# Two-layer graph network on one core: additions between the layers moved behind the next quotient, and two waits put inside GpSimd's groups of gathers

## The chip, the cores and the metric

The kernel runs on one core of one Trainium2 chip. A core has five engines that run their own instruction streams and meet only at semaphores: TensorE (PE), VectorE (DVE), ScalarE (ACT), GpSimd (POOL) and SyncE (SP), which here only issues DMAs. The metric is the device time of one execution in microseconds (us), lower is better.

## The reference

A graph has 6250 nodes with 128 features and 106250 edges sorted by their target node; every node has an edge to itself. Two layers run one after the other, each on the layer-normed and rectified nodes:

```
h = relu(layernorm(x))
# layer 0, per edge and feature
msg = h[src] + edge_attr
e = exp(beta*msg - segment_max(beta*msg, dst)[dst])
agg = segment_sum(msg * e / segment_sum(e, dst)[dst], dst)
x = x + (agg @ H + bias + h)            # H from phm_rule and W
# layer 1, four heads of 32 features
Wx = h @ W.T
logit = leaky_relu(Wx[src].a_left + Wx[dst].a_right, 0.2)
out = segment_sum(softmax_by_dst(logit) * Wx[src], dst)
x = x + elu(out)
```

## The kernel before, in words

The edges are cut into 208 groups of 512 (four blocks of 128 edges, one edge on each partition). Both layers are a software pipeline over the groups. Each engine runs the same list of stages, every stage with a fixed lag in groups; `sweep` (line 17) writes the first groups out, then a loop that is unrolled over 8 groups (`RING`), then the last ones. Nothing plans the order at run time: each engine does its instructions as written and waits at semaphores that count finished groups.

**Layer 0, group g.** GpSimd issues four indirect DMAs (`gather0`, line 655), which fetch the rows `h[src]` from DRAM into one of four buffers `ring_h` (`HRING` = 4). Before the first block it waits until ScalarE has lifted group g-4 out of that buffer (`lifted`). ScalarE copies the rows to PSUM (`lift0`, line 811), VectorE adds the edge features that SyncE has loaded (`add0`, line 1135), TensorE transposes the sum (`turn0`, line 1392), VectorE runs a scan forward and one backward for the maximum of each target node (`maxima0`, lines 1112 and 1117), and TensorE turns the maxima back and subtracts them in PSUM (`unturn0`, lines 1398 and 1402, two groups behind `turn0`). The end of `unturn0` increments `unturned`. ScalarE takes exponentials, VectorE the products, TensorE multiplies by one-hot matrices (line 1383) to sum over the target nodes, and ScalarE merges the sums into `acc`.

**Between the layers** the 6250 nodes are 13 batches of 512 (the last has 106). For batch b GpSimd makes a near quotient (`near0`), ScalarE copies it to PSUM (`lift_near0`, line 830), and VectorE finishes the division (`quotient0(b)`, line 1171, which increments `mid_agg`). TensorE multiplies by H (`layer_out(b)`, lines 1435 and 1440), one batch after the other into two PSUM places: it waits for `mid_agg` of its batch and for `self_res` of batch b-2. VectorE then adds the result to the nodes (`finish0(b)`, line 1177, which increments `self_res`) and takes the statistics for the next layernorm (four instructions of line 963). `lift_near0(b)` waits for the quotient of batch b-2, and GpSimd's `near0(b)` for the lift of batch b-4. Then VectorE makes the normed rows (`above1`), TensorE the products with W (`layer_in`, line 1462), and SyncE stores them to DRAM.

**Layer 1, group g.** GpSimd gathers from that table (`gather1`, line 683) into eight buffers; VectorE forms the logits when the four blocks have landed (`logits1`, line 1258); TensorE transposes them one group later (`turn1`, line 1492, which increments `msgT`); VectorE scans for the maxima; the rest is as before. VectorE also makes the one-hot matrices (`one_hot1`, line 1096).

In this text "block 2 of group g" is the third gather of a group, since blocks count from 0.

Of the kernel before, what the change touches and what calls it, by code (L numbers as in the profile page):

```python
# [44 lines left out]
def apart(eng):  # L45


    eng.nop(nofuse=True)


def later(item, n):

    return not isinstance(item, int) or item >= n


def gnn_kernel(nc, x_in, src_in, dst_in, ea_in, rule_in, w0_in, bias_in, beta_in, w1_in, a_in, out):
# [15 lines left out]
    NBAT = -(-NT // GB)  # L72
# [18 lines left out]
    with ctx:  # L91
# [225 lines left out]
        L0, L1 = layer_sems(0), layer_sems(1)  # L317
# [27 lines left out]
        def logs(b):  # L345
            if b < SPARE_LOGS:
                return (pos, elu_e, fin)[b // 2][:, b % 2, :]
            return onehot[:, b - SPARE_LOGS, :, :].rearrange("p b n -> p (b n)")
# [4 lines left out]
        def near_bank(b):  # L353
            return bank[b % 2]
# [21 lines left out]
        def real_rows(g, b):  # L376
            if isinstance(g, int) and g == NG - 1:
                return max(0, min(P, E - (g * GE + b * P)))
            return P
# [7 lines left out]
        def last(stage, back, **where):  # L387
            g = NG - 1 - back
            stage(g, g % RING, g // RING, **where)
# [197 lines left out]
        def _(pool):  # L587
# [52 lines left out]
            def gather0(g, s, use):  # L640
                if isinstance(g, int) and g < HALF:
                    pool.wait_ge(first_src, 16)
                    if g == 2:
                        pool.wait_ge(key_out, len(TABLE_BANKS))
                elif s < HALF:
                    pool.wait_ge(L0["listed"][0], 16 * use)
                else:
                    pool.wait_ge(L0["listed"][1], 16 * (use + 1))
                if later(g, HRING):
                    pool.wait_ge(L0["lifted"], g - (HRING - 1))  # L650
                apart(pool)
                for b in range(GB):
                    n = real_rows(g, b)
                    if n:
                        pool.indirect_dma_start(hg[0:n, s % HRING, b, :], None, h_dram,  # L655
                                                bass.IndirectOffsetOnAxis(ap=meta_g[0:n, s, b:b + 1], axis=0)
                                                ).then_inc(L0["gathered"][s % HRING], 16)

            sweep_edges(pool, [(0, gather0)])

            pool.wait_ge(pool_sum, len(POOL_SUMS))
# [13 lines left out]
            def gather1(g, s, use):  # L675
                pool.wait_ge(L1["listed"][s // HALF], 16 * (use + 1))
                if later(g, RING):
                    pool.wait_ge(L1["multiplied"], g - (RING - 1))
                apart(pool)
                for b in range(GB):  # L680
                    n = real_rows(g, b)
                    if n:
                        pool.indirect_dma_start(msg[0:n, s, b, :], None, wx_dram,  # L683
                                                bass.IndirectOffsetOnAxis(ap=meta_g[0:n, s, b:b + 1], axis=0)
                                                ).then_inc(L1["gathered"][s], 16)

            for u in range(WXB):
                pool.wait_ge(wx_stored[u], 16 * ((NBAT - 1 - u) // WXB + 1))
            sweep_edges(pool, [(0, gather1)])


# [255 lines left out]
        def _(dve):  # L947
# [218 lines left out]
            def quotient0(b):  # L1166
                w = LAST if b == NBAT - 1 else GE
                dve.wait_ge(mid_quot, b + 1)
                dve.wait_ge(mid_lifted, b + 1)
                rows = logs(b)[:, 0:w]  # L1170
                dve.scalar_tensor_tensor(rows, near_bank(b)[:, 0:w], 2.0, rows, ALU.subtract, ALU.mult).then_inc(mid_agg, 1)

            def finish0(b):
                t, rows = extent(b)
                dve.wait_ge(mid_out, b + 1)
                tiles = nodes[0:rows, b * GB:b * GB + t, :]
                dve.tensor_tensor(tiles, tiles, sums[0:rows, 1, b % 2, 0:t * D].rearrange("p (t d) -> p t d", d=D), ALU.add
                                  ).then_inc(self_res, 1)
                dve.wait_ge(self_res, b + 1)
                statistics(b)  # L1180
# [8 lines left out]
            last(products0, 1)  # L1189
            quotient0(0)  # L1190
            last(products0, 0)
            quotient0(1)
            dve.wait_ge(dve_sum, len(DVE_SUMS))
            dve.wait_ge(pool_sum, len(POOL_SUMS))
            quotient0(2)
            quotient0(3)
            for b in range(NBAT):
                if b + 4 < NBAT:
                    quotient0(b + 4)
                finish0(b)  # L1200
            dve.wait_ge(measured, 2 * NBAT)

# [355 lines left out]
```

## Time and profile before

| what | value |
|---|---|
| time, median of 3 runs | 2254.29 us (2253.85 to 2254.93) |
| the profiled execution's own time | 2258.94 us |
| its span, first to last instruction | 2257.2 us |
| layer 0, first to last gather's start | 36.97 to 1075.76 us |
| layer 1, first to last gather's start | 1165.09 to 2209.11 us |
| TensorE, VectorE, ScalarE, GpSimd busy | 86%, 88%, 63%, 73% |

The share of busy time is an average; which engine bounds a stage is read from who waits for whom in it. A row of the timeline gives the start in us from the span's start, the busy time in us, engine, line, operation, output and inputs, and in square brackets the idle time of that engine just before it and what ended it.

### The profile page before, as it was taken

How to read it: one execution, taken by the hardware profiler on the slowest of the kernel's cores; microseconds unless marked ns; L12 is line 12 of the kernel's file. 1: busy time of each engine (PE TensorE's matmuls, PEld its weight loads, DVE VectorE, ACT ScalarE, POOL GpSimd, SP SyncE). 2: the span in 40 equal slices, each digit the busy share in tenths (PEclk: the TensorE clock that was granted, in tenths of full speed). 3: DMA queues.
4: the chain of work that ended last, by engine and by line, in shares of the span. 5: the costliest groups of instructions: out<-in, count | busy, mean ns of one | idle time of the engine just before them, and what ended most of it. 6: DMA issues, size and time to landing. Idle time of an engine off the chain costs nothing.

```text
span 2257.2 us, 61657 instructions
## 1 busy us (share of the span) xinstructions
PE 1940.5 (86%) x14541; PEld 1712.6 (76%) x14542; DVE 1986.2 (88%) x3873; ACT 1419.4 (63%) x3494; POOL 1644.8 (73%) x1739
## 2 busy tenths in 40 slices
PE   2888888888888888888879999999999899899997
PEld 1777777777777767777768888888888888888886
DVE  7999999999999999999759889888888888888886
ACT  3677777776777677777635555555555555555556
POOL 5777777777777777777527777777777777777775
PEclk9999999999999999999768989999999999999998
DMA  6444444444444444443023333333333333333331
GB/s 214 128 126 137 132 132 136 123 132 132 137 132 132 128 133 132 133 136 112 6 81 61 60 59 59 59 58 59 59 59 58 58 59 59 59 59 59 58 59 68
DMA packets 318697, 213.52 MB, mean 95 GB/s; under 512 B 169938, under 2 KB 279074, under 8 KB 318642
## 3 DMA queue, kind: packets, MB, share of 16 engines
q0 software_dynamic: 53184, 112.31, 20.8%
q1 hardware_dynamic: 264608, 100.15, 17.1%
q8 instruction: 23, 0.38, 0.1%
q10 hardware_dynamic: 850, 0.43, 0.1%
q14 instruction: 32, 0.26, 0.0%
HBM read 200.69 MB, written 10.29 MB: 93 GB/s over the span
## 4 chain that ended last, share of the span: by engine, by line
POOL 45%; issue 21%; DMA 13%; DVE 9%; PE 5%; ACT 5%; SPq 1%; ACTq 1%; POOLq 1%; DVEq 0%
POOL msg L683 25%; POOL ring_h L655 19%; DMA ring_h<-h_dram,meta_g 10%; DMA msg<-wx_dram,meta_g 3%; DVE seg_max L1117 2%; DVE sums L1112 2%; ACT banks L811 2%; PE sums L1383 1%; DVE onehot L1096 1%; PE sums L1440 1%; DVE prod L1281 1%; ACT acc L777 1%; SPq L556 1%; POOL wgt L703 0%; ACT sums L797 0%
## 5 line engine op out<-in xcount | busy, mean ns | idle before, releaser
L683 POOL DMA_INDIRECT msg<-wx_dram,meta_g x831 | 791.8, 953 | 304.4 <-issue 246.1
L655 POOL DMA_INDIRECT ring_h<-h_dram,meta_g x831 | 786.6, 947 | 265.7 <-issue 244.8
L1383 PE MATMUL sums<-onehot,prod 128*128 128x128 f32 x3296 | 686.4, 292 | 17.7 <-issue 5.9
L1383 PE MATMUL sums<-onehot,wgt 128*128 128x128 f32 x3296 | 668.9, 286 | 0.0
L1383 PEld LDWEIGHTS sums<-onehot,prod 128*128 128x128 f32 x3296 | 531.1, 203 | 52.0 <-issue 51.2
L1383 PEld LDWEIGHTS sums<-onehot,wgt 128*128 128x128 f32 x3296 | 532.5, 203 | 0.0
L777 ACT ACTIVATE acc<-sums 128x1022 f32 x410 | 419.9, 1024 | 0.1
L811 ACT ACTIVATE banks<-ring_h,sign 128x512 f32<-128x512 f32 x208 | 143.9, 692 | 266.8 <-DMA ring_h<-h_dram,meta_g 259.2
L1402 PEld LDWEIGHTS sums<-neg_ident,seg_max 128*128 128x128 f32 x1664 | 220.1, 193 | 100.5 <-issue 100.0
L1392 PE MATMUL banks<-ident,msg 128*128 128x128 f32 x832 | 137.4, 288 | 160.0 <-DVE msg L1135 159.9
L1112 DVE TENSOR_TENSOR_SCAN sums<-flags,seg_max,banks 4x512 f32<-4x512 bf16 x207 | 264.1, 1276 | 5.8 <-PE banks L1492 4.0
L1112 DVE TENSOR_TENSOR_SCAN banks<-flags,seg_max,banks 128x512 f32<-128x512 bf16 x207 | 264.6, 1278 | 0.0
L1117 DVE TENSOR_TENSOR_SCAN seg_max<-flags,banks 128x512 f32<-128x512 bf16 x208 | 253.9, 1221 | 7.2
L1117 DVE TENSOR_TENSOR_SCAN seg_max<-flags,sums 4x512 f32<-4x512 bf16 x208 | 251.2, 1208 | 7.1
L1392 PEld LDWEIGHTS banks<-ident,msg 128*128 128x128 f32 x832 | 89.0, 142 | 198.1 <-issue 182.7
L769 ACT ACTIVATE carried<-acc,scale 128x2 f32 x414 | 121.3, 293 | 170.7 <-PE sums L1383 147.2
L1402 PE MATMUL sums<-neg_ident,seg_max 128*128 128x128 f32 x1664 | 220.7, 276 | 0.0
L1483 PEld LDWEIGHTS banks<-window,onehotT 128*128 128x128 f32 x1664 | 211.4, 199 | 9.3 <-issue 9.3
L1135 DVE SCALAR_TENSOR_TENSOR msg<-msg,sign,banks 128x512 f32<-128x512 f32 x208 | 155.3, 747 | 71.3 <-ACT banks L811 60.4
L1398 PE MATMUL sums<-msg,ident 128*128 128x512 f32 x416 | 215.1, 599 | 1.9 <-ACT sums L797 1.8
L1483 PE MATMUL banks<-window,onehotT 128*128 128x4 f32 x1664 | 205.6, 247 | 8.3 <-DMA window<-wx_dram 7.9
L902 ACT ACTIVATE sums<-logit_d 128x16 f32<-128x16 f32 x208 | 39.0, 188 | 260.4 <-DVE logit_d L1273 258.2
(215 smaller groups left out, 2887.4 us busy)
## 6 DMA issues: line engine op xcount, KB each, us to landing
msg<-in_edge_attr SPq DMA_DIRECT2D x207, 256.0 KB
flags<-flag_dram SPq DMA_DIRECT2D x52, 512.2 KB
window<-wx_dram SPq DMA_DIRECT2D x832, 2.0 KB
ring_h<-h_dram,meta_g POOLq DMA_INDIRECT x831
msg<-wx_dram,meta_g POOLq DMA_INDIRECT x831
wx_dram<-msg SPq DMA_DIRECT2D x13, 272.0 KB, 2.1
nodes<-in_x SPq DMA_DIRECT2D x6, 512.0 KB, 6.5
h_dram<-acc SPq DMA_DIRECT2D x12, 256.0 KB
```

Source lines behind the costliest of these rows:

```text
L655: pool.indirect_dma_start(hg[0:n, s % HRING, b, :], None, h_dram, bass.IndirectOffsetOnAxis(ap=meta_g[0:n, s, b:b + 1], axis=0)).then_inc( ...
L683: pool.indirect_dma_start(msg[0:n, s, b, :], None, wx_dram, bass.IndirectOffsetOnAxis(ap=meta_g[0:n, s, b:b + 1], axis=0)).then_inc(L1["ga ...
L777: act.activation(acc[:, :, bass.ds(node + 1, WIN - 1)], where[:, :, 1:WIN], ACT.Copy).then_inc(k["merged"], 1)
L811: act.activation(row_psum, ring_h[:, s % HRING, :], ACT.Copy, scale=sign[:, 0:1]).then_inc(L0["lifted"], 1)
L1112: dve.tensor_tensor_scan(run, flag[:, 0:GE], data, before, ALU.add, ALU.max).then_inc(k["scanned"], 1)
L1117: dve.tensor_tensor_scan(seg_max[0:n, par, ::-1], flag[:, GE:0:-1], run[:, ::-1], -BIG, ALU.add, ALU.max).then_inc(k["scanned"], 1)
L1135: dve.scalar_tensor_tensor(msg[:, s, :, 0:D], msg[:, s, :, 0:D], sign[:, 0:1], row_psum.rearrange("p (b d) -> p b d", b=GB), ALU.mult, ALU.add
L1383: ins = pe.matmul(where[:, j, bass.ds(off, P)], what[:, slot, b, :], onehot[:, s, b, :], start=(b == 0), stop=(b == GB - 1), skip_group_ch ...
L1392: ins = pe.transpose(bank[s % 2][:, b * P:(b + 1) * P], msg[:, s, b, 0:D], ident[:, :])
L1398: pe.matmul(shift_psum.rearrange("p (b d) -> p b d", b=GB), ident[:, :], msg[:, s, :, 0:D], start=True, stop=False, skip_group_check=True)
L1402: ins = pe.matmul(shift_psum[:, b * P:(b + 1) * P], seg_max[:, s % 2, b * P:(b + 1) * P], neg_ident[:, :], start=False, stop=(b == GB - 1) ...
L1483: ins = pe.matmul(bank[1][:, b * H:(b + 1) * H], onehotT[:, s % 2, b * P:(b + 1) * P], window[:, s, b, :], start=True, stop=True)
```

## The change

Three edits. In layer 0, from group 4 on, GpSimd waits before block 2 of group g until TensorE has finished `unturn0` of group g-4. In layer 1, from group 2 on, it waits before block 3 of group g until TensorE has finished `turn1` of group g-2. Each wait is followed by an empty instruction (`apart`), which keeps it from being joined to the DMA. Between the layers VectorE no longer makes four quotients ahead of the first `finish0`: it makes one, and then `quotient0(b + 1)` and `finish0(b)` in turn.

```diff
                 for b in range(GB):
+                    if b == 2 and later(g, 4):
+                        pool.wait_ge(L0["unturned"], g - 3)
+                        apart(pool)
                     n = real_rows(g, b)
...
                 for b in range(GB):
+                    if b == 3 and later(g, 2):
+                        pool.wait_ge(L1["msgT"], g - 1)
+                        apart(pool)
                     n = real_rows(g, b)
...
             last(products0, 0)
-            quotient0(1)
             dve.wait_ge(dve_sum, len(DVE_SUMS))
             dve.wait_ge(pool_sum, len(POOL_SUMS))
-            quotient0(2)
-            quotient0(3)
             for b in range(NBAT):
-                if b + 4 < NBAT:
-                    quotient0(b + 4)
+                if b + 1 < NBAT:
+                    quotient0(b + 1)
                 finish0(b)
```

GpSimd in the loop of layer 0, before: the end of one group of gathers and the next group. `lifted0` and `unturned0` are the semaphores of layer 0, `listed0_0` that of the index lists.

```order
L650 REGISTER_ALU [waits listed0_0]
L655 DMA ring_h<-h_dram,meta_g 128x128 [waits lifted0]
L655 DMA ring_h<-h_dram,meta_g 128x128 x3
L650 REGISTER_ALU [waits listed0_0]
L655 DMA ring_h<-h_dram,meta_g 128x128 [waits lifted0]
L655 DMA ring_h<-h_dram,meta_g 128x128 x3
```

The same place of the changed kernel (its lines are 3 to 6 further down):

```order
L650 REGISTER_ALU [waits listed0_0]
L658 DMA ring_h<-h_dram,meta_g 128x128 [waits lifted0]
L658 DMA ring_h<-h_dram,meta_g 128x128
L658 DMA ring_h<-h_dram,meta_g 128x128 [waits unturned0]
L658 DMA ring_h<-h_dram,meta_g 128x128
L650 REGISTER_ALU [waits listed0_0]
L658 DMA ring_h<-h_dram,meta_g 128x128 [waits lifted0]
L658 DMA ring_h<-h_dram,meta_g 128x128
```

The order of the gathers is the same; the third of each four has a wait of its own.

VectorE between the layers, before: the first two rows are `quotient0(0)` and the last product of layer 0, `pos`, `elu_e` and `fin` rows of line 1171 are the quotients of batches 1 to 4.

```order
L1171 SCALAR_TENSOR_TENSOR pos<-banks,pos 128x512 [waits mid_lifted,mid_quot]
L1147 TENSOR_TENSOR prod<-sums,msg 128x512 [waits weighed0,summed0]
L1171 SCALAR_TENSOR_TENSOR pos<-banks,pos 128x512 [waits mid_lifted,mid_quot]
L1171 SCALAR_TENSOR_TENSOR elu_e<-banks,elu_e 128x512 [waits mid_quot,mid_lifted,pool_sum,dve_sum]
L1171 SCALAR_TENSOR_TENSOR elu_e<-banks,elu_e 128x512 [waits mid_lifted,mid_quot]
L1171 SCALAR_TENSOR_TENSOR fin<-banks,fin 128x512 [waits mid_lifted,mid_quot]
L1177 TENSOR_TENSOR nodes<-nodes,sums 128x512 [waits mid_out]
L963 BN_STATS stats<-nodes 128x6 [waits self_res]
```

The same place of the changed kernel, where line 1177 is now the quotient and line 1183 the addition of `finish0`:

```order
L1177 SCALAR_TENSOR_TENSOR pos<-banks,pos 128x512 [waits mid_lifted,mid_quot]
L1153 TENSOR_TENSOR prod<-sums,msg 128x512 [waits weighed0,summed0]
L1177 SCALAR_TENSOR_TENSOR pos<-banks,pos 128x512 [waits mid_quot,mid_lifted,pool_sum,dve_sum]
L1183 TENSOR_TENSOR nodes<-nodes,sums 128x512 [waits mid_out]
L969 BN_STATS stats<-nodes 128x6 [waits self_res]
L969 BN_STATS stats<-nodes 128x6 x3
L1177 SCALAR_TENSOR_TENSOR elu_e<-banks,elu_e 128x512 [waits mid_lifted,mid_quot]
L1183 TENSOR_TENSOR nodes<-nodes,sums 128x512 [waits mid_out]
```

The first addition stands behind the quotient of batch 1 instead of that of batch 4, and from there on quotients and additions alternate, three batches closer together than before.

## Rows read from the trace of the kernel before

**Rows 1.** The page, busy us (share of the span) of each engine

```profile
PE 1940.5 (86%) x14541; PEld 1712.6 (76%) x14542; DVE 1986.2 (88%) x3873; ACT 1419.4 (63%) x3494; POOL 1644.8 (73%) x1739
```

**Rows 2.** Groups by line, GpSimd: busy us, mean ns, idle before and its enders

```profile
L655 POOL DMA_INDIRECT ring_h<-h_dram,meta_g x831 | 786.6, 947 | 265.7 <-issue 244.8 <-DMA h_dram<-acc 12.6 <-ACT banks L811 7.9
L683 POOL DMA_INDIRECT msg<-wx_dram,meta_g x831 | 791.8, 953 | 304.4 <-issue 246.1 <-DMA wx_dram<-msg 51.2 <-DVE prod L1281 7.0
```

**Rows 3.** The waits: us in total, times, longest us

```profile
ACT banks L811 <- DMA ring_h<-h_dram,meta_g: 259.2, 197, 3.5
...
POOL msg L683 <- issue: 246.1, 807, 0.3
POOL ring_h L655 <- issue: 244.8, 803, 0.3
```

**Rows 4.** Timeline of GpSimd, layer 0: block 2 of groups 4, 39, 200

```profile
60.15 0.94 POOL L655 DMA_INDIRECT ring_h<-h_dram,meta_g  x1 [0.30 <-issue]
...
235.24 0.95 POOL L655 DMA_INDIRECT ring_h<-h_dram,meta_g  x1 [0.30 <-ACT banks L811]
...
1040.74 0.95 POOL L655 DMA_INDIRECT ring_h<-h_dram,meta_g  x1 [0.31 <-issue]
```

**Rows 5.** Timeline of TensorE, layer 0: end of unturn0, groups 0, 35, 196

```profile
61.26 1.91 PE L1402 MATMUL sums<-neg_ident,seg_max 128*128 128x128 f32 x8
...
234.29 1.59 PE L1402 MATMUL sums<-neg_ident,seg_max 128*128 128x128 f32 x8
...
1038.87 1.05 PE L1402 MATMUL sums<-neg_ident,seg_max 128*128 128x128 f32 x8
```

**Rows 6.** Timeline of GpSimd, layer 1: block 3 of group 9

```profile
1214.10 0.94 POOL L683 DMA_INDIRECT msg<-wx_dram,meta_g  x1 [0.30 <-issue]
```

**Rows 7.** Timeline of TensorE, layer 1: turn1 of group 7

```profile
1212.63 0.60 PE L1492 MATMUL banks<-ident,logit 128*4 128x128 f32 x4
```

**Rows 8.** Timeline of TensorE between the layers: layer_out 0 to 3, 12, first turn_h

```profile
1098.01 0.38 PE L1435 MATMUL sums<-bias_rows,ones_rows 3*128 3x512 bf16 x1
...
1100.39 0.38 PE L1435 MATMUL sums<-bias_rows,ones_rows 3*128 3x512 bf16 x1
...
1104.68 0.38 PE L1435 MATMUL sums<-bias_rows,ones_rows 3*128 3x512 bf16 x1 [1.84 <-DVE nodes L1177]
...
1107.16 0.60 PE L1435 MATMUL sums<-bias_rows,ones_rows 3*128 3x512 bf16 x1
...
1131.46 0.34 PE L1435 MATMUL sums<-bias_rows,ones_rows 3*106 3x128 bf16 x1
...
1135.28 1.97 PE L1451 MATMUL banks<-ident,hn 128*128 128x128 f32 x8 [2.79 <-DVE hn L1213]
```

**Rows 9.** Timeline of VectorE between the layers: first addition and its neighbours

```profile
1103.34 0.69 DVE L1171 SCALAR_TENSOR_TENSOR fin<-banks,fin 128x512 f32<-128x512 f32 x1 [2.47 <-ACT banks L830]
1103.94 0.68 DVE L1177 TENSOR_TENSOR nodes<-nodes,sums 128x512 f32<-128x512 f32 x1
...
1105.51 0.67 DVE L1171 SCALAR_TENSOR_TENSOR fin<-banks,fin 128x512 f32<-128x512 f32 x1
```

**Rows 10.** Windows: length, busy of PE, PEld, DVE, ACT, POOL, granted clock, DMA

```profile
1104.70:1107.10 2.40, 2.40 (x9) 2.00 (x9) 2.27 (x8) 2.03 (x5) 2.32 (x3) 0.73 0.01 3
1107.10:1109.80 2.70, 2.70 (x10) 2.04 (x9) 2.60 (x10) 0.66 (x2) 2.62 (x3) 0.50 0.01 3
...
1140.60:1146.00 5.40, 5.34 (x24) 5.35 (x25) 3.63 (x14) 2.14 (x7) 0.00 (x0) 0.50 0.21 77
```

**Rows 11.** Timeline of TensorE, layer 0: turn0 behind two equal idle times

```profile
231.80 0.98 PE L1392 MATMUL banks<-ident,msg 128*128 128x128 f32 x4 [1.89 <-DVE msg L1135]
...
712.05 0.65 PE L1392 MATMUL banks<-ident,msg 128*128 128x128 f32 x4 [1.87 <-DVE msg L1135]
```

**Rows 12.** Timeline, layer 1: a long block 0 and the one-hots beside it

```profile
1511.53 0.86 DVE L1096 TENSOR_SCALAR onehot<-iota_f,meta_g 128x128 f32<-128x128 f32 x4
1511.94 1.07 POOL L683 DMA_INDIRECT msg<-wx_dram,meta_g  x1 [0.31 <-issue]
```

## The prediction

> **What bounds the kernel now.** I read the page's busy shares first. VectorE has 88% and TensorE 86%, GpSimd only 73% [rows 1], so by that view the change touches an engine with room. The groups by line say otherwise: 831 gathers of layer 0 take 947 ns each and those of layer 1 953 ns [rows 2], and the table of waits puts GpSimd's idle time before them down to its own issue, over 800 times in each layer and never longer than 0.3 us [rows 3]. 947 ns and 305 ns of idle time (265.7 us less the 12.6 us before the first gather, over 830 gathers [rows 2]) make 1.252 us a gather and 5.01 us a group of four; 207.75 groups make 1040 us, the whole stretch from the first gather to the last. GpSimd is thus never late because of anybody, and the others wait for it: ScalarE stood 259.2 us before its lift, at 197 of 208 groups, until a gather landed [rows 3]. Both sweeps end when GpSimd's stream ends, and a delay of that stream anywhere is a delay of the whole. Between the layers GpSimd is idle for 51.2 us until the new table is stored [rows 2]; there the chain through VectorE and TensorE sets the time, and a gain in it moves layer 1 forward one to one.
>
> So two of the three edits sit on the engine that bounds, and can only cost unless something else moves; the third sits on the chain between.
>
> **The wait in layer 0.** A wait that is already met costs nothing: block 0 of each group has two waits, a register instruction and an empty one ahead of it, blocks 1 to 3 have none, and no gather of either layer had more than 0.3 us of idle time for its own issue [rows 3]. What counts is whether `unturn0` of group g-4 is done when block 2 of group g would start. In steady state it is: at group 200, the closest of groups 12 to 206 but for 39 and 40, TensorE ends at 1038.87 + 1.05 = 1039.92 [rows 5] and block 2 starts at 1040.74 [rows 4], 0.82 us later; half of these 195 groups have 1.5 us or more. At the start it is not. Block 2 of group 4 starts at 60.15 [rows 4], but `unturn0` of group 0 ends at 61.26 + 1.91 = 63.17 [rows 5], since VectorE and TensorE enter the sweep late, behind the setup. GpSimd loses 3.02 us and a release, which I take as 0.2 us. Queued behind the wait are only further gathers; ScalarE's lift of group 4 waits for them. Groups 5 to 9 would also have been early in the trace, each by less than group 4, so the one delay covers them, while `unturn0` of groups 1 to 3 depends on gathers that are issued before it. Group 39 is the one other case: TensorE stood idle for 1.89 us, came back at the lower of its two clocks (its four transposes took 0.98 us instead of 0.65) [rows 11], and ended at 234.29 + 1.59 = 235.88 [rows 5] against 235.24 [rows 4], 0.64 us too late. Whether that falls there again is chance; another idle time of 1.87 us was not followed by it [rows 11]. Bounds for the wait in layer 0: 3.0 us (release for nothing, no second event) to 3.2 + 8 x 0.85 = 10.0 us, if eight groups meet a slow `unturn0` and each costs 0.64 us and a release. I take 3.2, nearest to the one sure row. Below 3.0 it can't go, as nothing in the change makes `unturn0` of group 0 earlier.
>
> **The wait in layer 1.** The closest group is 9: `turn1` of group 7 ends at 1212.63 + 0.60 = 1213.23 [rows 7], block 3 of group 9 starts at 1214.10 [rows 6], 0.87 us later. All other 204 groups have more, most 2 to 3 us. Cost nothing, hidden by the lead of two groups. If that cover were gone by a slow TensorE, about 0.85 us an event as above.
>
> **The quotients between the layers.** `layer_out` starts at 1098.01, 1100.39, 1104.68 and 1107.16 [rows 8]. The first two follow each other by 2.38 us, TensorE's own pace at the full clock. The third comes 1.84 us late, and what ended the wait is the first addition (`self_res`), which stood on VectorE behind the quotient of batch 4: that quotient waited 2.47 us for ScalarE and ran from 1103.34, the addition from 1103.94 to 1104.62 [rows 9]. In the changed order the addition of batch 0 stands behind quotient 1, which VectorE makes long before. It starts when `layer_out(0)` ends, at 1100.45. From it to the next quotient's start are 1105.51 - 1103.94 = 1.57 us, and the quotient takes 0.68 [rows 9], so batch 2 is ready at 1100.45 + 0.04 + 1.57 + 0.68 = 1102.74, and with 0.06 us of release (1104.62 to 1104.68) at 1102.80. `layer_out(1)` ends at 1100.39 + 2.38 = 1102.77. The gap closes: 1104.68 - 1102.80 = 1.88 us gained. From there on the round VectorE must make for each batch is 0.04 + 1.57 + 0.68 + 0.06 = 2.35 us, against TensorE's 2.38: just inside. ScalarE's lifts and GpSimd's near quotients lose their lead of several batches, but a lift needs only the quotient two batches back, and GpSimd's near quotients the lift four back, so I cost them at nothing.
>
> The second part of the gain is the clock. TensorE is granted the full clock up to this place, and 0.73 in the window of `layer_out(2)`, then 0.50 for all that follow [rows 10]; the pace goes from 2.38 to 2.70 us. From 1104.68 on TensorE had no idle time, so the gap of 1.84 us ahead of it is the nearest cause in the trace. Batches 2 to 11 took 1131.46 - 1104.68 = 26.78 us [rows 8]; at 2.38 they take 23.8. If the clock holds, 3.0 us more are gained, 4.9 in all; if it falls at the same place all the same, 1.9 in all. For holding speaks that idle times of 1.87 us inside layer 0 left the clock alone [rows 11]; against it, that layer 0 has much denser work around such a gap. I take holding, a little likelier. Bounds of the edit: 0 (if VectorE's round of 2.35 us turns out longer than the lower clock's 2.70, the gap is only spread out) to -7.6 (below).
>
> The Trainium skill, "TensorE: Matmul & The Clock Gate", section "What's actually happening", says: "the default state is throttled, and activity releases the throttle." By that rule the closed gap favours the full clock; but these batches ran 25 us without idle time and stayed at 0.50 [rows 10], so busy time in the trace is not what it counts. By the rule read on busy time alone the sum would be the one with the clock held.
>
> **Sum.** +3.2 (layer 0) + 0 (layer 1) - 4.9 (between) = -1.7 us. On the profiled execution's own time that is 2258.94 - 1.7 = 2257.2; that execution stands 4.65 us above the median of the runs, and the comparison is with the median: 2254.3 - 1.7 = 2252.6 us. Changes under 0.2%, 4.5 us, count as no change for this kernel.
>
> **The rivals.**
> - *The clock falls as before.* +3.2 - 1.9 = +1.3: 2255.6 us. For it: the low density of these batches, whose lower clock never recovered. Against: the gap is gone.
> - *The clock holds through the next step too.* Two batches of `turn_h` and `layer_in` took 5.40 us at clock 0.50 [rows 10]; at the full clock half of that, 2.7 us less. -1.7 - 2.7 = -4.4: 2249.9. Against: TensorE is idle for 2.79 us before [rows 8], while VectorE makes the norms.
> - *GpSimd falls behind TensorE again and again (the other side).* Place: block 2 in layer 0. Before, four buffers let GpSimd run on past a slow `unturn0`; now every one stops it, and each stop delays the landing for which TensorE then waits idle, which may cost it its clock once more. Price 0.85 us an event; with 1.3 us from the start it passes +4.5 from the fourth event on; with eight it is +1.3 + 6.8 = +8.1: 2262.4. For it: group 39. Against: one event in 195 groups, and the closest others at 0.82 us.
> - *The gain between the layers doesn't come.* If the later quotients arrive late on TensorE, the gap is only spread out: +3.2 alone, 2257.5. For it: 2.35 against 2.38 is thin. Against: at the lower clock 2.70 leaves room.
> - *Layer 1 loses a stall.* Its gathers take 6 ns more on average than layer 0's [rows 2], 5 us in all; the excess is in block 0, as the one of 1.07 us beside four one-hots of VectorE [rows 12]. A shift of GpSimd against VectorE could remove it: -1.7 - 5 = -6.7, 2247.6. Against: the wait in layer 1 never binds, and VectorE's one-hots follow the landing of GpSimd's own gathers, so nothing shifts. The Trainium skill, "SBUF — State Buffer", section "Who interferes with whom", has the rule for this: a VectorE instruction in a two-port mode and GpSimd lock each other out of a shared pair of ports. By it the stall would stay wherever the two still meet.
>
> **How the numbers follow.** Forecast 0.40; clock falls as before 0.25; clock holds on 0.07; repeated stops 0.17; no gain between 0.08; layer 1 loses its stall 0.03. Faster by over 0.2%: the last, half of "holds on" and a little of the forecast's tail, 0.10. Slower by over 0.2%: most of the repeated stops and the tails of the two cases above zero, 0.22. Within 0.2%: 0.68. The range of the forecast itself is 2250.5 to 2255; the range for eight in ten goes from 2249.5 (holds on) to 2260.5, through the first half of the repeated stops.
>
> **What would show it.** Right: GpSimd's first idle time above 0.3 us at block 2 of group 4, about 3.3 us long and ended by TensorE's line 1402, and at most a few more; none in layer 1; the last gather of layer 0 about 3.2 us later after the first; `layer_out` at even steps of 2.38 us with clock 1.0, and some 84.4 us instead of 89.3 between the last gather of layer 0 and the first of layer 1. Wrong: many idle times ended by TensorE in layer 0, gathers in layer 1 that wait, a step above 2.7 us in `layer_out`, or a mean of a gather other than 947 and 953 ns.

## The result and the profile after

| | before | after |
|---|---|---|
| time, median of 20 runs each | 2253.86 us (2251.85 to 2256.03) | 2256.82 us (2255.26 to 2259.04) |
| ratio | | 1.0014, 95% interval 1.0008 to 1.002 |
| the profiled execution's own time | 2258.94 us | 2257.39 us |
| its span | 2257.2 us | 2255.6 us |

The changed kernel is 3.0 us slower; the forecast was 1.7 us faster. By the bound of 0.2% (4.5 us) both are no change, but the interval of the ratio lies wholly above 1, so the sign was wrong. 2256.82 us lies outside the range of the forecast itself (2250.5 to 2255) and inside the wider one for eight in ten (2249.5 to 2260.5). The two profiled executions say the opposite of the 40 runs: 1.6 us shorter. Before's profiled execution stands 5.1 us above its median, higher than any of its 20 runs; after's stands 0.6 us above. -1.6 + 5.1 - 0.6 = +2.9, which is the measured difference. So differences between these two traces are good for finding where something happens, not for its size to a microsecond.

By the starts of the gathers, layer 0 took 1042.38 us instead of 1038.79, the stretch between the layers 84.68 instead of 89.33, and layer 1 1043.37 instead of 1044.02.

The waits of GpSimd in the changed kernel (what it waited for: us in total, times, longest us), beside [rows 3]:

```profile
POOL msg L689 <- issue: 219.6, 717, 0.9
POOL ring_h L658 <- issue: 218.6, 717, 0.4
POOL msg L689 <- DMA wx_dram<-msg: 45.9, 1, 45.9
POOL msg L689 <- PE banks L1495: 34.4, 113, 0.3
POOL ring_h L658 <- PE sums L1405: 28.6, 76, 3.5
```

TensorE is named in 76 idle times of layer 0, but nearly all are the usual 0.3 us between two gathers. In the timeline of all gathers only four idle times in layer 0 (block 2 of groups 4, 39, 44 and 199) and two in layer 1 pass 0.36 us; before there was none. Block 2 of group 4, with the product it waited for, is the first of these pairs; block 2 of group 39 and block 2 of group 199 are the others (start us, us, engine, line, output and inputs, idle before and its ender):

```profile
61.66 1.36 PE L1405 MATMUL sums<-neg_ident,seg_max 128*128 128x128 f32 x8
236.61 1.92 PE L1405 MATMUL sums<-neg_ident,seg_max 128*128 128x128 f32 x8
1037.58 1.50 PE L1405 MATMUL sums<-neg_ident,seg_max 128*128 128x128 f32 x8
```

```profile
63.77 0.94 POOL L658 DMA_INDIRECT ring_h<-h_dram,meta_g  x1 [3.54 <-PE sums L1405]
239.28 0.94 POOL L658 DMA_INDIRECT ring_h<-h_dram,meta_g  x1 [1.01 <-PE sums L1405]
1039.83 0.94 POOL L658 DMA_INDIRECT ring_h<-h_dram,meta_g  x1 [1.84 <-PE sums L1405]
```

TensorE ends at 61.66 + 1.36 = 63.02, 238.53 and 1039.08; the gathers start at 63.77, 239.28 and 1039.83. Each is 0.75 us later. That is the release of a gather by TensorE, and the prediction had put it at 0.2 us. With the 0.30 us that each gather has anyway, the three cost 3.24, 0.71 and 1.54 us.

In layer 1 block 3 of group 2 stood 0.88 us. The first row is `turn1` of group 0, for which it waits:

```profile
1174.80 1.01 PE L1495 MATMUL banks<-ident,logit 128*4 128x128 f32 x4
1178.85 0.94 POOL L689 DMA_INDIRECT msg<-wx_dram,meta_g  x1 [0.88 <-issue]
```

The other idle time of layer 1, 0.73 us at block 1 of group 160, stands where the change has no wait.

TensorE between the layers in the changed kernel: the starts of `layer_out` for batches 0 to 4 and 12, and the first `turn_h`, beside [rows 8], and ahead of them TensorE's last idle time before it:

```profile
1100.05 0.46 PE L1386 MATMUL sums<-onehot,prod 128*128 128x128 f32 x2 [1.85 <-ACT acc L783]
...
1102.01 0.39 PE L1438 MATMUL sums<-bias_rows,ones_rows 3*128 3x512 bf16 x1
1104.38 0.38 PE L1438 MATMUL sums<-bias_rows,ones_rows 3*128 3x512 bf16 x1
1106.89 0.37 PE L1438 MATMUL sums<-bias_rows,ones_rows 3*128 3x512 bf16 x1
1109.27 0.37 PE L1438 MATMUL sums<-bias_rows,ones_rows 3*128 3x512 bf16 x1
1111.76 0.58 PE L1438 MATMUL sums<-bias_rows,ones_rows 3*128 3x512 bf16 x1
...
1133.34 0.34 PE L1438 MATMUL sums<-bias_rows,ones_rows 3*106 3x128 bf16 x1
...
1137.16 1.97 PE L1454 MATMUL banks<-ident,hn 128*128 128x128 f32 x8 [2.79 <-DVE hn L1216]
```

And the windows of that stretch (the window, its length, the busy us of PE, PEld, DVE, ACT and POOL, the granted clock, the DMA share, GB/s), beside [rows 10]:

```profile
1106.90:1109.30 2.40, 2.40 (x10) 2.04 (x10) 2.12 (x6) 1.88 (x5) 1.64 (x2) 1.00 0.01 3
1109.30:1111.80 2.50, 2.50 (x11) 2.05 (x10) 2.15 (x6) 1.34 (x4) 2.42 (x3) 0.68 0.00 0
1111.80:1133.30 21.50, 21.50 (x73) 16.25 (x72) 16.80 (x48) 3.78 (x7) 6.11 (x7) 0.50 0.00 1
1137.10:1142.50 5.40, 3.92 (x16) 3.36 (x16) 4.88 (x26) 1.29 (x4) 0.00 (x0) 0.65 0.00 0
1142.50:1150.00 7.50, 7.45 (x62) 7.11 (x63) 7.26 (x28) 5.67 (x20) 0.00 (x0) 1.00 0.39 147
```

The gap of 1.84 us is gone: the third batch starts 2.51 us after the second, not 4.29. But the clock fell all the same, around 1110 us, after ten us in which TensorE had only 0.06 us of idle time (at 1106.89), so the closed gap is not what the clock hung on; from there on the step is 2.70 us as before. It then came back earlier: the first step of `turn_h` at the full clock begins at 1142.55, before at 1146.04. From the first to the last `layer_out` are 31.33 us instead of 33.45, and from the first `turn_h` to layer 1's first gather 27.29 instead of 29.81. The 4.65 us by which this stretch is shorter in this pair of traces are thus 2.1 us from the closed gap and a later fall of the clock, and 2.5 us from its earlier return.

### The profile page after: what moved, and what is told of

It reads as the page before. It is cut to its first block, busy times and chain, and to the rows that moved or that the text cites. A ratio compares the mean times of both kernels' runs of the same rounds, so it can differ in the third digit from the quotient of the medians.

```text
span 2255.6 us, 62211 instructions
## 1 busy us (share of the span) xinstructions
PE 1937.2 (86%) x14541; PEld 1708.8 (76%) x14542; DVE 1986.9 (88%) x3873; ACT 1418.0 (63%) x3494; POOL 1641.2 (73%) x1739
## 4 chain that ended last, share of the span: by engine, by line
POOL 22%; issue 22%; DVE 18%; PE 17%; DMA 15%; ACT 4%; SPq 1%; DVEq 1%; POOLq 1%; ACTq 0%
POOL ring_h L658 13%; DMA ring_h<-h_dram,meta_g 9%; POOL msg L689 9%; DVE seg_max L1123 5%; DMA msg<-wx_dram,meta_g 5%; DVE sums L1118 4%; PE sums L1386 4%; ACT banks L817 2%; PE banks L1495 2%; PE sums L1405 2%; PE sums L1401 2%; DVE msg L1141 2%; PE banks L1395 1%; PE banks L1504 1%; DVE banks L1118 1%
```

## The experiments

Sixteen runs were made in four sessions, each on another chip. In one session the kernel before took 2258.56 us, near the 2253.86 of the comparison above. In the other three it took 3347.35, 3315.95 and 3309.45 us. I call the first kind the fast chip and the other the slow chips; ratios hold within a session only. A difference in us below is (ratio - 1) times the time of before. Neither wait was run alone on a fast chip, so what each costs there is read from traces.

| kernel | chip: before, us | median, us | ratio, 95% interval |
|---|---|---|---|
| whole change | fast: 2258.56 | 2263.43 | 1.002 (1.001 to 1.0029) |
| both waits, no quotient edit | fast: 2258.56 | 2266.62 | 1.0038 (1.0024 to 1.0052) |
| whole change, layer 0 wait from group 8 | fast: 2258.56 | 2259.46 | 1.0005 (0.9996 to 1.0014) |
| quotient edit alone | fast: 2258.56 | 2258.55 | 0.9996 (0.9987 to 1.0005) |
| quotient edit alone | slow: 3347.35, 3315.95 | 3347.85, 3304.89 | 1.0005 (0.9977 to 1.0033), 0.9987 (0.9955 to 1.002) |
| layer 0 wait alone | slow: the same two | 3192.92, 3182.97 | 0.9549 (0.9513 to 0.9586), 0.9612 (0.9571 to 0.9653) |
| layer 1 wait alone | slow: the same two | 3187.55, 3127.45 | 0.9527 (0.9493 to 0.9561), 0.942 (0.9392 to 0.9448) |
| layer 0 wait alone, from group 8 | slow: 3347.35 | 3206.93 | 0.9571 (0.9535 to 0.9607) |
| whole change | slow: 3309.45 | 3004.5 | 0.9074 (0.9038 to 0.911) |
| whole change, both waits from group 8 | slow: 3309.45 | 3029.42 | 0.9155 (0.9117 to 0.9193) |
| the same, each wait one group looser | slow: 3309.45 | 3023.95 | 0.9139 (0.9102 to 0.9175) |
| whole change without the two waits | slow: 3309.45 | 3319.04 | 1.0006 (0.9973 to 1.004) |

**The quotient edit alone**, in three sessions. The edit is the last part of the change:

```diff
-            quotient0(1)
...
-            quotient0(2)
-            quotient0(3)
             for b in range(NBAT):
-                if b + 4 < NBAT:
-                    quotient0(b + 4)
+                if b + 1 < NBAT:
+                    quotient0(b + 1)
                 finish0(b)
```

> The kernel before with the new order of quotients and additions alone. Theory A (the steps as in the two traces: the gap on TensorE between the layers closes, the clock falls a little later): 1.9 us faster than before if the clock falls at the same place, up to 4.9 us if it holds. Theory B (the profiled execution of before was one with an early fall of the clock, and its usual execution has less to gain): no more than 1.9 us faster, and perhaps nothing. In the trace layer 1's first gather should come 85 us after layer 0's last, against 89.3 us.

> The new order of quotients and additions alone, once more, for a chip like the first one. Theory A: 1.9 us faster than before, as far as the closed gap goes, and up to 4.9 us if the usual execution of before also has its clock fall early. Theory B (the additions' order does not matter in the usual execution): within 1 us of before.

> The quotient edit alone. If the kernel before is near 2254 us: theory A (the gap of 1.84 us in TensorE's products closes): -1.9 us, the clock falling as before, or -4.9 us if it holds. Rival B (the gap is spread out over the following batches): 0 us. If the kernel before is near 3300 us: nothing that can be measured, as twice before.

On the fast chip it gave -0.9 us (-2.9 to +1.1), not the -4.9 of the forecast, and told neither from zero (rival B) nor from the -1.9 of theory A. In the trace layer 1's first gather comes 87.47 us after layer 0's last, not the 85 expected. On the slow chips it measured nothing, as the third text expected. `layer_out` of the first five batches there:

```profile
1099.73 0.60 PE L1432 MATMUL sums<-bias_rows,ones_rows 3*128 3x512 bf16 x1
1102.33 0.38 PE L1432 MATMUL sums<-bias_rows,ones_rows 3*128 3x512 bf16 x1
1104.84 0.37 PE L1432 MATMUL sums<-bias_rows,ones_rows 3*128 3x512 bf16 x1
1107.22 0.37 PE L1432 MATMUL sums<-bias_rows,ones_rows 3*128 3x512 bf16 x1
1109.71 0.37 PE L1432 MATMUL sums<-bias_rows,ones_rows 3*128 3x512 bf16 x1
```

The first row has the low clock (0.60 us instead of 0.38), the next four the full one, and the sixth batch the low one again. In each of the six traces of fast chips it falls at another place.

**Both waits without the quotient edit**, on the fast chip: the change without the diff above.

> Both waits without the quotient edit. If the kernel before is near 2254 us: theory A (the waits cost the stall at group 4 and two or three late blocks, 3.2 us + 0.7 to 2 us, and the quotient edit gives back about 1.9 us): +4 to +6 us, so 1 to 3 us above the whole change. Rival B (the waits cost 3.2 us and the quotient edit gives nothing): +3 us, like the whole change. If the kernel before is near 3300 us: the same ratio as the whole change within 0.3%, since the quotient edit alone measured 1.0005 and 0.9987 there.

It measured +8.6 us (+5.4 to +11.7), above both theories. The idle times above 0.36 us that its trace has at the new waits come to 4.8 us, so about 4 us stay unexplained. The whole change, with the quotient edit, measured 4.1 us less, more than the 0.9 that the edit gives alone; with such intervals the two do not contradict each other, and the worth of the edit is known only to some 2 us. Its `layer_out` for batches 0 to 3 shows one case in which the old order of quotients costs little:

```profile
1103.26 0.60 PE L1441 MATMUL sums<-bias_rows,ones_rows 3*128 3x512 bf16 x1
1105.96 0.60 PE L1441 MATMUL sums<-bias_rows,ones_rows 3*128 3x512 bf16 x1
1109.03 0.60 PE L1441 MATMUL sums<-bias_rows,ones_rows 3*128 3x512 bf16 x1 [0.30 <-DVE nodes L1183]
1111.73 0.60 PE L1441 MATMUL sums<-bias_rows,ones_rows 3*128 3x512 bf16 x1
```

With TensorE at its low clock from the start, the addition that came 1.84 us late in [rows 8] comes 0.30 us late: the slower batches cover the rest. By these traces, one execution each, the edit is worth about 2 us where the clock is full there (first to last batch 33.45 us before, 31.33 after) and 0.4 us where it is not (32.77 in this kernel, 32.40 in the next).

**The wait of layer 0 from group 8 on**, with the rest of the change, on the fast chip; and on a slow chip alone.

```diff
-                    if b == 2 and later(g, 4):
+                    if b == 2 and later(g, 8):
```

> The whole change with the wait of layer 0 from group 8 on, so that the wait for the late start of TensorE in group 4 is gone. If the kernel before is near 2254 us: theory A (the stall at group 4 is a delay of the whole stream): 3 us below the whole change, so about 0 to -0.5 us against the kernel before. Rival B (the stall at group 4 is covered, because GpSimd would have to wait for the same engines later in any case): like the whole change, +3 us. If the kernel before is near 3300 us: no difference to the whole change that can be measured (3 us in 3000).

> The kernel before with layer 0's wait from group 8 on instead of group 4. Theory A: the 3.2 us of group 4 are gone, and 0.3 to 2 us remain for groups with a slow unturn0. Theory B (the wait costs in every group): as much slower as with the wait from group 4 on, less 3.2 us, so still 3 us or more.

On the fast chip this is 3.4 us below the whole change (1.0005 against 1.002, each known to some 2 us), as theory A said; all eleven executions lie below the median of the whole change's ten. In the traces layer 0 took 1038.84 us instead of 1040.88. The stall at group 4 is a delay of the whole stream. What takes its place is smaller. The two idle times of layer 0 above 0.36 us:

```profile
80.45 0.94 POOL L658 DMA_INDIRECT ring_h<-h_dram,meta_g  x1 [0.84 <-PE sums L1405]
101.87 0.94 POOL L658 DMA_INDIRECT ring_h<-h_dram,meta_g  x1 [1.75 <-PE sums L1405]
```

and the products they waited for:

```profile
78.65 1.05 PE L1405 MATMUL sums<-neg_ident,seg_max 128*128 128x128 f32 x8
99.50 1.62 PE L1405 MATMUL sums<-neg_ident,seg_max 128*128 128x128 f32 x8
```

79.70 to 80.45 and 101.12 to 101.87: 0.75 us again, now in a second kernel on another chip. On the slow chip the wait from group 8 on gained as much as from group 4 on (0.9571 and 0.9549), where both theories had expected a loss.

**The whole change again**, on the fast chip and on a slow one.

> The whole change once more, to see its sum beside its parts on one chip. Two cases, told apart by the time of the kernel before in this call. If that is near 2254 us, as in the first comparison: +3.0 us (ratio 1.0014), with GpSimd's first stall at block 2 of group 4 about 3.3 us long. If it is near 3300 us, as in the two calls so far, theory A (there each wait shortens its own layer by 130 to 180 us and the two add up, since the waits alone gave 0.955 to 0.961 and 0.942 to 0.953): ratio 0.90 to 0.92. Rival B (the stalls that a wait takes away in one layer come from a shared cause and come back elsewhere): ratio 0.94 to 0.96, no better than one wait alone.

> The whole change, as the thing to compare with in this call. If the kernel before is near 2254 us: +3 to +4.5 us, as measured twice. If it is near 3300 us: theory A (the two waits' gains add up) 0.90 to 0.92; rival B (they don't) 0.94 to 0.96.

On the fast chip it repeats the sign: +4.5 us (+2.3 to +6.5). The stall at group 4 took 4.09 us there, since `unturn0` of group 0 was at the low clock (1.91 us instead of 1.36). The execution with that trace took 2257.15 us, the fastest of the ten and 6.3 below their median, so the trace need not hold all of the +4.5. On the slow chip the same kernel is 9.3% faster, 305 us.

**Each wait alone**, on two slow chips: one of the first two parts of the change without the rest.

> The kernel before with the wait inside layer 0's groups alone. Theory A (only waits that are not met cost): 3.2 us slower for group 4, and 0.7 to 1.5 us for each group whose unturn0 ran at TensorE's lower clock, of which the trace of the changed kernel has two; so 3.2 to 6 us slower. Theory B (each wait costs a little by itself): over 6 us slower, with the mean gather longer or the idle time before it above 0.305 us throughout.

> The kernel before with the wait inside layer 1's groups alone. Theory A: 0 to 1 us slower, since the changed kernel's trace has one idle time of 0.89 us at block 3 of group 2 and one other. Theory B (each wait costs a little by itself): 2 us slower or more.

> Layer 0's wait alone, once more. On a chip where before takes 2254 us: 3.2 to 6 us slower (theory A: group 4, and groups whose unturn0 ran at the lower clock). On a chip where before takes 3300 us: 4 to 5% faster again, all of it within layer 0.

> Layer 1's wait alone, once more. On a chip where before takes 2254 us: 0 to 1 us slower (theory A). Theory B (a wait costs a little by itself in each group): 2 us slower or more. On a chip where before takes 3300 us: 4 to 5% faster again, all of it within layer 1.

The first two expectations had no gain of any kind: on a slow chip each wait makes the kernel 4 to 6% faster. The last two, written after that, had 4 to 5%; the wait in layer 0 gave 3.9% and the one in layer 1 5.8%. Each wait shortens its own layer and changes the other by at most 17 us. The gathers of the quotient edit alone, of the wait in layer 0 alone and of the wait in layer 1 alone, by line in the first of these sessions (duration in ns, least, median, largest; first and last start in us):

```profile
L655 POOL DMA_INDIRECT ring_h<-h_dram,meta_g x831: 883/947/1196, 37.6 to 1584.9; - x167
L683 POOL DMA_INDIRECT msg<-wx_dram,meta_g x831: 880/947/1097, 1684.9 to 3261.4; - x167
```

```profile
L658 POOL DMA_INDIRECT ring_h<-h_dram,meta_g x831: 887/944/1198, 37.5 to 1452.5; - x167
L686 POOL DMA_INDIRECT msg<-wx_dram,meta_g x831: 872/944/1097, 1541.0 to 3100.5; - x167
```

```profile
L655 POOL DMA_INDIRECT ring_h<-h_dram,meta_g x831: 887/944/1203, 37.5 to 1585.8; - x167
L686 POOL DMA_INDIRECT msg<-wx_dram,meta_g x831: 872/944/1094, 1688.5 to 3132.1; - x167
```

Layer 0 takes 1547, 1415 and 1548 us; layer 1 takes 1577, 1560 and 1444. A gather itself takes its 944 to 947 ns as on the fast chip.

**The kernel before on a slow chip**, to see what bounds it there.

> The kernel before itself, for a second trace of it. Theory A (the profiled execution of before was unusual: 2258.94 us against 2253.86 us at the median of 20 runs): if this chip is like the first one, this trace differs from the first one in TensorE's clock between the layers, with less than 89.3 us from layer 0's last gather to layer 1's first. Theory B (that execution was usual where it matters): 89 us again, with the clock at 0.50 from the third layer_out on. On a chip like the second one (before at 3347 us), neither is told apart.

It took 3295.78 us, so by its own words this run tells neither theory apart. Its busy shares, and the three largest waits of ScalarE's line 769 and GpSimd's gathers:

```profile
PE 2368.1 (72%) x14541; PEld 2118.3 (64%) x14542; DVE 2008.0 (61%) x3873; ACT 1419.3 (43%) x3494; POOL 1642.2 (50%) x1739
```

```profile
ACT carried L769 <- remote: 671.5, 159, 6.8
POOL ring_h L655 <- ACT banks L811: 417.9, 95, 7.6
POOL msg L683 <- DVE prod L1281: 415.1, 119, 7.6
```

VectorE, ScalarE and GpSimd are busy as long as in [rows 1]; what is added is idle time on all of them. TensorE is another matter: it is busy for 2368.1 us instead of 1940.5, at a mean granted clock of 0.784 instead of 0.948. GpSimd does not bound here: it runs ahead and then stands until ScalarE or VectorE frees a buffer. Its gathers around 600 us:

```profile
603.22 0.95 POOL L655 DMA_INDIRECT ring_h<-h_dram,meta_g  x1 [0.30 <-issue]
610.35 0.94 POOL L655 DMA_INDIRECT ring_h<-h_dram,meta_g  x1 [6.19 <-ACT banks L811]
613.34 0.94 POOL L655 DMA_INDIRECT ring_h<-h_dram,meta_g  x1 [2.04 <-issue]
...
620.82 0.94 POOL L655 DMA_INDIRECT ring_h<-h_dram,meta_g  x1 [0.30 <-issue]
626.47 0.94 POOL L655 DMA_INDIRECT ring_h<-h_dram,meta_g  x1 [4.71 <-ACT banks L811]
```

ScalarE's own idle time before line 769 is put down to "remote", 671.5 us in 159 pieces: the table names no instruction for it. The semaphore updates in the trace do. Each of the 159 ends with an update of `summed`, which only TensorE's line 1383 makes. In the wait shown below, TensorE's last product of the group is shown as ended at 616.82 us, and the update comes at 623.25. In the trace of before on the fast chip every recorded update of TensorE's counters of groups comes within 0.02 us of the end of its product; here, in layer 0, those of `summed` come 4.2 us after it at the median and up to 6.8. So it is TensorE that finishes late, and the others wait for it. The low clock does not explain that by itself: 527 of the 671.5 us fall where the granted clock was 1.00, as in this wait of ScalarE from 616.6 to 623.4 us (columns as in [rows 10]):

```profile
616.80:623.20 6.40, 2.20 (x15) 1.53 (x12) 3.45 (x5) 0.00 (x0) 3.77 (x4) 1.00 0.62 174
```

What holds TensorE up, no run shows.

**The empty instructions without the waits**, on a slow chip:

```diff
                     if b == 2 and later(g, 4):
-                        pool.wait_ge(L0["unturned"], g - 3)
                         apart(pool)
...
                     if b == 3 and later(g, 2):
-                        pool.wait_ge(L1["msgT"], g - 1)
                         apart(pool)
```

> The whole change without its two waits: the empty instructions ahead of block 2 and block 3 stay, and so does the quotient edit. If the kernel before is near 2254 us: theory A (an empty instruction is hidden in the 0.30 us between two gathers): like the quotient edit alone, 0 to -2 us. If the kernel before is near 3300 us: theory A (waits help because they hold GpSimd back to TensorE's pace): ratio 1.00, no gain. Rival B (what helps is only the space between two DMA instructions): 0.90 to 0.96, as with the waits.

1.0006: the gain needs the waits, not the space between instructions. Rival B falls. Theory A's condition holds, no gain without the waits; that they help by keeping GpSimd to TensorE's pace is not shown by this run.

**Both waits from group 8 on, tight and one group looser**, on the same slow chip:

```diff
-                    if b == 2 and later(g, 4):
-                        pool.wait_ge(L0["unturned"], g - 3)
+                    if b == 2 and later(g, 8):
+                        pool.wait_ge(L0["unturned"], g - 4)
...
-                    if b == 3 and later(g, 2):
-                        pool.wait_ge(L1["msgT"], g - 1)
+                    if b == 3 and later(g, 8):
+                        pool.wait_ge(L1["msgT"], g - 2)
```

> The whole change with both waits from group 8 on. If the kernel before is near 2254 us: theory A (what the waits cost are the blocks at which TensorE was later than 0.75 us before GpSimd's start: those at group 4 of layer 0 and at groups 2 to 6 of layer 1, 3.5 and 0.7 to 1.4 us in the four traces so far): 4 to 5 us below the whole change, -2 to +1 us against before, and no idle time over 0.36 us in the first eight groups of either layer. Rival B (the waits cost something at every group): within 2 us of the whole change. If the kernel before is near 3300 us: 0.90 to 0.92 if the two waits' gains add up, 0.94 to 0.96 if not.

> Both waits from group 8 on, each for one group earlier than in the change (unturn0 of group g-5, turn1 of group g-3), and the quotient edit. If the kernel before is near 2254 us: theory A (only late blocks cost): no stall of GpSimd at all, so the quotient edit alone, 0 to -2 us, and 0 to 2 us below the kernel with the same waits one group tighter. If the kernel before is near 3300 us: theory A (the tight lead is what spreads the gathers): the gain shrinks, ratio above that of the tight waits by 0.01 or more. Rival B (any bound below the ring's does it): same ratio as the tight waits within 0.005.

0.9155 and 0.9139: the same within their intervals, so between these two bounds it does not matter how tight the wait is, as rival B said, and the gains of the two layers add up (0.955 to 0.961 and 0.942 to 0.953 alone). The waits of the whole change on that chip, for comparison with the three lines above:

```profile
ACT carried L775 <- remote: 419.7, 100, 7.0
...
POOL ring_h L658 <- remote: 223.0, 100, 2.8
...
POOL ring_h L658 <- PE sums L1405: 190.7, 52, 4.6
```

That idle time of ScalarE falls from 671.5 to 419.7 us when GpSimd is held back in shorter stops (in layer 0 the longest is 4.6 us instead of 7.6; stops above 1 us are 151 and 147). The updates of `summed` in layer 0 then come 0.84 us after the product at the median, not 4.2: TensorE is held up less. Whether the bursts of gathers hold it up or only go with it, these runs do not show. None of the last four kernels was run on a fast chip but the whole change, so what the waits from group 8 on cost there in layer 1 is not measured.

## Why the prediction was wrong, point by point

- *What bounds.* Right on the fast chips: with the wait from group 4 on, layer 0 took 1042.38, 1040.88 and 1042.86 us, without it 1038.79 and 1039.01, and taking away the stall at group 4 gave 3.4 us back.
- *A met wait costs nothing.* Right in layer 0 and in layer 1's steady state: GpSimd's idle times stay at 0.30 us there.
- *The wait in layer 0, +3.2 us.* The place was right (block 2 of group 4 first, then 39), the price too low. The release takes 0.75 us and not 0.2. By [rows 4, 5] that makes 63.17 + 0.75 - 60.15 = 3.77 us for group 4; the three traces with that wait lost 3.24, 3.79 and 3.54. It also shrinks the cover: a lead of 0.82 us at group 200 was in truth one of 0.07, and in the changed kernel the group beside it was late. The prediction also had groups 5 to 9 early in its trace; there block 2 is 1.45, 0.84 and 0.40 us too early for groups 5 to 7 and 0.05 and 0.44 late enough for 8 and 9, which changes nothing in the sum. Layer 0 lost 5.55 us to such idle times in the first trace (3.24, 0.71 and 1.54, and 0.07 at group 44) and 3.8 in each of the next two, where 0.2 us more stand at block 1 of group 184, ahead of which there is no wait.
- *The wait in layer 1, 0.* Wrong by 0.6 to 1.4 us, as far as traces show. In all four traces of the fast kind with it, block 3 of group 2 stood 0.85 to 1.37 us instead of 0.30. The profile names no cause, but in each of the four it starts 3.03 or 3.04 us after `turn1` of group 0 has ended (1175.81 to 1178.85 in the first), so it hangs on that product, by something longer than the release. The sequencer's rows say where the time goes: in the first trace it was past the wait at 1175.87, 0.05 us after the product, and reached its next wait, for an index list, 2.8 us later, where the same way took 0.54 us in groups 3 and 4. So the wait ends in time and the issue of the gather behind it is slow, once. Later blocks, of groups 3 to 6, were held in three of the four, 0.78 us behind their product. The cover that the prediction relied on, 0.87 us at the closest group, was that of one execution: in the trace of the quotient edit alone, without any wait, block 3 of groups 3, 4 and 6 starts 0.41, 0.09 and 0.72 us before `turn1` has ended.
- *The quotient edit, -4.9 us.* **The step that failed most.** Closing the gap worked as worked out: from the first `layer_out` to the third are 4.88 us instead of 6.67, 1.79 gained where 1.88 was forecast. Both things built on it did not. "Clock held", 3.0 us of the sum, fell: the clock fell at about 1110 us with only 0.06 us of idle time in the ten us before it, and in the other traces it stood low at the first batch, rose and fell again, or was full for three batches. And the gap of 1.84 us is there only where the clock is full; at the low clock it was 0.30. Measured, the edit gives -0.9 us (-2.9 to +1.1).
- *The basis.* The sum was made on an execution that stood 4.65 us above the median shown, and I carried its gap and its clock over as if they were the usual ones, while the whole sum was 1.7 us.
- *The sum with what the runs showed.* At blocks that have a new wait, the two traces of the whole change have 6.1 and 5.0 us of added idle time; with -0.9 for the quotient edit that is +5.2 and +4.1, against +3.0 and +4.5 measured. (The waits without the quotient edit have 4.8 us in the trace and measured +8.6.) A term that the prediction did not have works the other way: the gathers took 944 ns instead of 947 [rows 2] in layer 0 of each of the three traces of fast chips with the quotient edit and the waits, which is 831 x 2.3 ns = 1.9 us, and 951, 949 and 951 instead of 953 in layer 1. The prediction had named another mean as a sign against it. I have no cause for it; the kernel before has 944 in layer 0 on a slow chip, so it does not need the edits.
- *Luck.* The stretch between the layers took 84.68 us in the first trace, and 84.4 was forecast. The mechanism was not the forecast one: the clock fell and came back early. In the other traces with the quotient edit the stretch took 86.42, 86.26 and 87.47.
- *The rivals.* "The clock falls as before" was right in its mechanism; with the release corrected its +1.3 becomes +1.9 for the sure stalls and more with the rare ones. Repeated stops came two or three times, not eight. "The gain between the layers doesn't come", +3.2, is nearest to the measured +3.0 in number, but not in mechanism: the gap closed, and the waits cost more than 3.2. "Holds on" was half right in the first trace, by the early return of the clock at `turn_h`, without holding in between.

The Trainium skill, "TensorE: Matmul & The Clock Gate", section "What's actually happening", was weighed in the prediction for a clock held by steady activity. The first trace goes against it read that way: the fall came inside the 31.33 us from the first to the last `layer_out`, in which TensorE had 0.06 us of idle time. The prediction's own sentence, that these batches ran 25 us without idle time at 0.50, had said as much, and I did not act on it.

What stays open: what holds TensorE up on a slow chip, so that the kernel takes 1000 us longer, and why holding GpSimd back takes 9% off its time; and why the issue behind the first wait of layer 1 is slow. Why the whole change was better there than the same with both waits from group 8 on (0.9074 against 0.9155) can be placed: in the traces the first 16 groups of the two layers take 102.3 and 104.2 us with the whole change and 111.7 and 117.1 with the later waits, 22.3 us of the 24.7 between the two executions, and the longest stop, 13.2 us, is the first wait itself, at block 2 of group 8 of layer 0. The version with only the wait of layer 0 moved to group 8 is the best compromise seen: not to be told from before on the fast chip. On a slow one it was not run, but the whole change and the version with both waits from group 8 on, between which it lies, were 8 to 9% faster there.

## What to carry to other kernels

Compare a wait's lead with the release time and not with zero, and take the release from a row in which that pair of engines really waits. Don't spend a gain on the clock that rests on where it fell in one execution, least of all when the sum is smaller than the distance of that execution from the median. A wait that can only cost on the engine that bounds can gain on another chip, where that engine doesn't bound: look for its worth where the others are late. Where a table names nobody for a wait, compare the semaphore's update with the end of the instruction that makes it.

## What the runs showed of the hardware

- From TensorE's last product to the start of a waiting gather: 0.75 to 0.77 us in layer 0, in nine held gathers of four traces, and 0.78 us in layer 1, in four of three traces, the first wait of layer 1 left out (3.03 us).
- TensorE's granted clock fell to 0.50 at 1110 us in a stretch in which it had 0.06 us of idle time in ten us, and at another place in each of six executions of nearly the same instructions.
- The same kernel took 2258.56 us on one chip and 3309 to 3347 us on three others, with busy times of VectorE, ScalarE and GpSimd within about 1% (2008.0, 1419.3 and 1642.2 us against 1986.2, 1419.4 and 1644.8). What differs is TensorE: 2368.1 us busy against 1940.5, clock 0.784 against 0.948, and updates of `summed` that come 4.2 us behind the product at the median instead of 0.02 at most. The whole change cost 0.14 and 0.2% on the first kind and gained 9.3% on the second.
